# The routed experts' up product in split single precision, full slot tiles first, causal key rows in one product

## The reference

```
q, k, v = x Wq, (x Wdown) Wk_up, (x Wdown) Wv_up      16 heads of 16, rotary on 12 of the 16
x1 = layernorm(x + softmax(causal(q k' / 4)) v)
scores = softmax(x1 gate')                              16 experts, the best two of each token
y = sum over the two chosen experts e of  w_e * ((silu(x1 w1[e]') * (x1 w3[e]')) w2[e]')    176 inner columns
z = the same product with one shared expert of 352 inner columns
out = layernorm(x1 + y + z)
```

## Time and profile before

| | us |
|---|---|
| median of three runs | 795.77 (789.0 to 796.28) |
| the profiled execution | 791.07 |
| its span, first to last instruction | 789.3 |
| PE busy in the span | 705.3 (89%) |
| DVE, ACT, POOL busy | 561.8, 395.3, 242.8 |
| PE's share of the chain that ended last | 71% |

### The profile page before, as it was taken

One profiled execution on the slowest core, in us unless ns is written; L12 is line 12 of the kernel. 1 busy time (PEld: TensorE's weight loads), 2 busy tenths in 40 slices (PEclk: granted clock), 3 DMA queues, 4 the chain that ended last, 5 costly groups with the idle time before them and its releaser, 6 DMA issues.

```text
span 789.3 us, 13246 instructions
## 1 busy us (share of the span) xinstructions
PE 705.3 (89%) x4150; PEld 468.9 (59%) x4151; DVE 561.8 (71%) x1279; ACT 395.3 (50%) x848; POOL 242.8 (31%) x297
## 2 busy tenths in 40 slices
PE   3589899899999999999999999999999799999910
PEld 3577575565766566556645565554477677777700
DVE  6666679978879977786798888753676655555545
ACT  2225465556656566666665777656823222222204
POOL 6426173440081207011511000010166513333332
PEclk9759799999999999999999999999999999999965
DMA  4854215043015101500421274522342133333254
GB/s 138 214 161 112 79 42 147 27 129 90 1 44 146 55 1 42 121 1 1 121 61 64 64 242 161 153 69 56 89 115 98 61 87 103 107 107 107 87 186 159
DMA packets 45096, 75.94 MB, mean 96 GB/s; under 512 B 5695, under 2 KB 23359, under 8 KB 44863
## 3 DMA queue, kind: packets, MB, share of 16 engines
q1 hardware_dynamic: 37423, 57.55, 26.9%
q0 software_dynamic: 4896, 13.67, 5.0%
q10 hardware_dynamic: 2720, 4.00, 1.4%
HBM read 41.91 MB, written 32.93 MB: 95 GB/s over the span
## 4 chain that ended last, share of the span: by engine, by line
PE 71%; DVE 15%; issue 4%; DMA 4%; ACT 3%; ACTq 1%; POOL 1%; SPq 0%; POOLq 0%; DVEq 0%
PE banks_ps L1079 16%; PE banks_ps L1136 15%; PE banks_ps L1116 14%; PE banks_ps L1173 7%; DVE mx L1343 5%; PE banks_ps L1207 5%; PE banks_ps L994 3%; PE banks_ps L1084 2%; PE banks_ps L1186 2%; ACT probs L881 2%; PE banks_ps L1269 1%; PE banks_ps L1195 1%; DVE base L1777 1%; PE banks_ps L1220 1%; DMA q_stack<-m_rows 1%
## 5 line engine op out<-in xcount | busy, mean ns | idle before, releaser
L881 ACT ACTIVATE probs<-banks_ps 128x512 f32<-128x512 f32 (+3 forms) x640 | 302.4, 546 | 185.5 <-PE banks_ps L1116 169.2
L1343 DVE TENSOR_REDUCE mx<-banks_ps 128x1 f32<-128x512 f32 (+3 forms) x576 | 307.6, 593 | 66.1 <-PE banks_ps L1079 65.2
L1079 PE MATMUL banks_ps<-k_stack,q_stack 96*128 96x512 f32 (+3 forms) x832 | 249.8, 364 | 7.1 <-DMA q_stack<-kq_split 3.1
L1116 PE MATMUL banks_ps<-q_stack,k_stack 98*128 98x512 f32 (+3 forms) x640 | 242.1, 397 | 12.1 <-ACT probs L881 6.6
L1079 PEld LDWEIGHTS banks_ps<-k_stack,q_stack 96*128 96x128 f32 x832 | 150.9, 200 | 84.7 <-DVE mx L1343 36.4
L1116 PEld LDWEIGHTS banks_ps<-q_stack,k_stack 98*128 98x128 f32 x640 | 121.9, 194 | 50.5 <-ACT probs L881 28.2
L735 POOL TENSOR_SCALAR_AFFINE_SELECT probs<-probs 128x512 f32<-128x512 f32 x64 | 40.9, 639 | 333.7 <-ACT probs L881 333.5
L1136 PE MATMUL banks_ps<-probs,v_ones 128*17 128x512 f32 (+3 forms) x1280 | 133.9, 536 | 0.9 <-POOL probs L735 0.9
L791 POOL DMA_INDIRECT token_y<-ys,dest x47 | 45.6, 970 | 82.0 <-DVE ys L1753 79.2
L1136 PEld LDWEIGHTS banks_ps<-probs,v_ones 128*17 128x17 f32 x1280 | 29.5, 97 | 65.3 <-issue 38.5
L1337 DVE TENSOR_REDUCE mx<-banks_ps 128x4 f32<-128x512 f32 x64 | 44.2, 691 | 28.7 <-PE banks_ps L1084 27.2
(11 more groups left out here) (180 smaller groups left out, 690.1 us busy)
## 6 DMA issues: line engine op xcount, KB each, us to landing
kq_split<-kq_stage SPq DMA_DIRECT2D x32, 256.0 KB, 3.4
k_stack<-kq_split SPq DMA_DIRECT2D x8, 768.0 KB, 6.7
q_stack<-kq_split SPq DMA_DIRECT2D x32, 192.0 KB, 5.7
xg<-slot_x SPq DMA_DIRECT2D x47, 130.0 KB, 2.2
slot_x<-blank SPq DMA_DIRECT2D x11, 520.0 KB, 6.3
w_up_sb<-w_up SPq DMA_DIRECT2D x16, 352.0 KB
kq_split<-kq_stage SPq DMA_DIRECT2D x32, 128.0 KB, 3.3
x_raw<-xT SPq DMA_DIRECT2D x4, 512.0 KB, 5.5
```

What stands on the lines that cost most here:

```text
L881: nc.scalar.activation(probs[:, s % PROB_BUFS, h, off:CH], score_bank(n)[:, off:CH], ACT.Exp)\
L1079: ins = nc.tensor.matmul(dst[:, at:at + keys], q_stack[0:STACK, u % 4, h, tile * P:(tile + 1) * P], k_stack[0:STACK, pair, kb * CH + k0:kb ...
L1116: nc.tensor.matmul(score_bank(n)[:, off:CH], k_stack[:, 2 * g + h // 2, b * P:(b + 1) * P], q_stack[:, u % 4, h, off:CH], start=True, stop ...
L1343: last = nc.vector.tensor_reduce(mx[:, u % 2, h * TPC + tile, column:column + 1], bank_of(bank)[:, at:at + keys], AX.X, ALU.max)
```

## The change

1. **Up product of the routed loop.** It becomes a split product: six fp32r matmuls of 352 columns in place of two plain f32 ones. ACT copies each expert's up weights (704 columns) to their high part (`high_expert`), POOL writes the low part over the raw ones (`low_expert`): twelve experts at steps of units 14 and 15 (`SPLIT_AT`, after the step's last exponential), four beside items 2, 4, 6 and 8 of the shared expert. DVE makes the low part of each tile's rows (`low_rows`), and PE's up product waits for it.
2. **Memory.** The split weights take twice the room. The raw up weights are loaded in another order and at other steps, the last four during the shared expert; the down weights come in five loads after attention, the last of them (experts 12 to 15, 704 KB) after `experts_ready`, and PE waits for all five before the loop. The shared expert's down weights and the last chunk's input rows are loaded after the last score; their split is by ACT and then by DVE ahead of item 0 (`low_down`), where DVE did all of it beside unit 15. Sums are kept in the rows of x1 (`sum_of`), so `take_shared(b)` waits for the scatters of chunk b.
3. **Full slot tiles first.** The slot order is: tiles that the first 12 token tiles fill for sure, then their partly filled ones, then those the last chunk adds. `early_slots` has more to compute; the expert of each tile is counted in three pieces, beside items 2, 4 and 10, where it was one beside item 8; and the first 9 slot tiles (`SURE`) are loaded without waiting for the last chunk's scatters.
4. **Causal rows at once.** For a unit's own chunk, query tile i has one product over its (i+1)*128 keys: tile 3 in one bank, tiles 2 and 0 in another, tile 1 in a third, each bank with a mask product of 128, 256 and 128 columns.

```diff
-SHARED_BANKS = ((1, 3), (2,))
+OWN_BANKS = ((3,), (2, 0), (1,))
...
+        ends = np.cumsum([(i + 1) * P for i in OWN_BANKS[n]])
+        return [(i, 0, (i + 1) * P, int(end) - (i + 1) * P) for i, end in zip(OWN_BANKS[n], ends)]
...
+    SPLIT_ORDER = (0, 1, 12, 2, 3, 4, 13, 5, 6, 7, 14, 15, 8, 9, 10, 11)
+    EXPERT_UP_AT = tuple(first_step[UNITS - 3] + 3 + 5 * n for n in range(3)) + \
+        tuple(first_step[UNITS - 2] + 1 + 3 * n for n in range(4)) + tuple(first_step[UNITS - 1] + 1 + 2 * n for n in range(5))
+    SPLIT_AT = tuple(first_step[UNITS - 2] + 2 * n + 1 for n in range(6)) + (first_step[UNITS - 1],) + \
+        tuple(first_step[UNITS - 1] + 4 + 2 * n for n in range(5))
+    SPLIT_BESIDE = (2, 4, 6, 8)
...
+        w_up_raw = lay("w_up_raw", late, 0, [P, EXPERTS, 2, KT, 2 * INTER])
+        w_up = lay("w_up_split", late, 0, [P, EXPERTS, 2, KT, 2 * INTER], F32R)
+        w_dn = lay("w_dn_sb", late, 28928, [HALF, EXPERTS, 2, E])
+        yg = lay("yg", late, 0, [P, 2, TOP_K, TPC, E])
+        x_tok_last = lay("x_tok_last", late, 22528, [P, TPC, E])
+        dn_raw = lay("dn_raw", late, 23568, [P, NG, E])
+        shared_dn = [lay("dn_high", late, 24576, [P, NG, E], F32R), lay("dn_low", late, 23568, [P, NG, E], F32R)]
...
+        def sum_of(b):
+            return base_last if b == LAST_C else x1[0][:, b * TPC:(b + 1) * TPC, 0:E]
...
-            def load_expert_up(e):
-                sp.dma_start(w_up[:, e], t["w_up"][:, e]).then_inc(experts_loaded, 16)
+            def load_expert_up(n):
+                e = SPLIT_ORDER[n]
+                sp.dma_start(w_up_raw[:, e, 0], t["w_up"][:, e]).then_inc(up_loaded[n], 16)
...
-            sp.wait_ge(weights_low, 6)
+            sp.wait_ge(pe_scores, GH * NS)
+            sp.dma_start(dn_raw, t["s_dn"]).then_inc(shared_loaded, 16)
             sp.dma_start(x_tok[LAST_C], t["x"][LAST_C * CH:, :].rearrange("(i p) n -> p i n", p=P)).then_inc(tokens_loaded, 16)
-            sp.wait_ge(pe_scores, GH * NS)
-            load_expert_down(2, 6)
-            load_expert_down(6, 10)
-            sp.wait_ge(scattered, 16 * TOP_K * TT)
+            for n in range(4):
+                sp.wait_ge(pe_gate, 2 * n + 1)
+                load_expert_up(EXPERTS - 4 + n)
+                load_expert_down(3 * n, 3 * n + 3)
+            sp.wait_ge(experts_ready, 1)
+            load_expert_down(12, EXPERTS)
+            for c in range(LAST_C):
+                sp.wait_ge(scattered[c], 16 * TOP_K * TPC)
...
+            for j in range(SURE):
+                load(j, j % RING, j)
+            sp.wait_ge(scattered[LAST_C], 16 * TOP_K * TPC)
+            turns = (SLOTS - SURE) // UNROLL
+            with sp.Fori(0, turns) as turn:
+                for k in range(UNROLL):
+                    load(turn * UNROLL + (SURE + k), (SURE + k) % RING, SURE + k)
...
+            def low_expert(n):
+                e = SPLIT_ORDER[n]
+                pool.wait_ge(up_high, n + 1)
+                nc.gpsimd.tensor_tensor(w_up[:, e, 0], w_up_raw[:, e, 0], w_up[:, e, 1].bitcast(F32), ALU.subtract).then_inc(up_low, 1)
...
+                if s - 1 in SPLIT_AT:
+                    low_expert(SPLIT_AT.index(s - 1))
...
+            for n in range(len(SPLIT_AT), EXPERTS):
+                low_expert(n)
             pool.wait_ge(slots_ready, 2)
             scatter(x1[1], EARLY, range(TPC))
...
+            def high_expert(n):
+                e = SPLIT_ORDER[n]
+                act.wait_ge(up_loaded[n], 16)
+                nc.scalar.activation(w_up[:, e, 1], w_up_raw[:, e, 0], ACT.Copy).then_inc(up_high, 1)
...
+                    if h == 3 and s in SPLIT_AT:
+                        high_expert(SPLIT_AT.index(s))
...
+            act.wait_ge(shared_loaded, 16 * 5)
+            nc.scalar.activation(shared_dn[0], dn_raw, ACT.Copy).then_inc(weights_high, 1)
...
+                if n in SPLIT_BESIDE:
+                    high_expert(len(SPLIT_AT) + SPLIT_BESIDE.index(n))
...
-                if masked:
-                    ins = nc.tensor.matmul(dst.rearrange("p (i k) -> p i k", i=TPC), ident_b[:],
-                                           mask_b[:].unsqueeze(1).to_broadcast([P, TPC, P]), start=False, stop=True,
+                if own:
+                    first, last = parts[0][2] - P, parts[-1][3] + parts[-1][2]
+                    ins = nc.tensor.matmul(dst[:, first:last].rearrange("p (i k) -> p i k", k=P), ident_b[:],
+                                           mask_b[:].unsqueeze(1).to_broadcast([P, (last - first) // P, P]), start=False, stop=True,
...
-            def up(n, par, x_of, e):
-                for k in range(KT):
-                    last = nc.tensor.matmul(gate_ps[par][:, 0:2 * INTER], x_of(k), w_up[:, e, k, :],
-                                            start=(k == 0), stop=(k == KT - 1))
+            def up(n, par, e):
+                for m, (k, (a, w)) in enumerate(product(range(KT), PARTS)):
+                    last = nc.tensor.matmul(gate_ps[par][:, 0:2 * INTER], xg_t[:, par, a, k, :], w_up[:, e, 1 - w, k, :],
+                                            start=(m == 0), stop=(m == 3 * KT - 1))
...
-                    pe.wait_ge(experts_loaded, 16 * (EXPERTS + 5))
+                    pe.wait_ge(experts_loaded, 16 * 5)
+                    pe.wait_ge(up_low, EXPERTS)
...
-                pe.wait_ge(xt_copied, j + 1)
+                pe.wait_ge(xt_low, j + 1)
                 if j0 == 0:
                     pe.wait_ge(wide_hidden_done, SHARED)
-                up(j, j0 % 2, lambda k: xg_t[:, j0 % 2, k, :], bass.ds(own, 1))
+                up(j, j0 % 2, bass.ds(own, 1))
...
-                if kb == c and i == 0:
-                    nc.vector.tensor_reduce(mx[:, u % 2, h * TPC:(h + 1) * TPC, c:c + 1],
-                                            bank_of(bank).rearrange("p (i k) -> p i k", i=TPC), AX.X, ALU.max)\
-                      .then_inc(max_done, 1)
-                    return
-                column = kb if kb < c else c + 1
                 for tile, _, keys, at in bank_parts(bank):
-                    last = nc.vector.tensor_reduce(mx[:, u % 2, h * TPC + tile, column:column + 1],
+                    last = nc.vector.tensor_reduce(mx[:, u % 2, h * TPC + tile, kb:kb + 1],
...
+            def low_down():
+                dve.wait_ge(weights_high, 6)
+                nc.vector.tensor_tensor(shared_dn[1], dn_raw, shared_dn[0].bitcast(F32), ALU.subtract).then_inc(weights_low, 1)
...
+            def move_on(at, n):
+                link(nc.vector.tensor_tensor(grid[:, at], place[:, at], along_t(row_of(CAP), n), ALU.is_ge))
+                link(nc.vector.scalar_tensor_tensor(out=grid[:, at], in0=grid[:, at], scalar=float(P),
+                                                    in1=along_t(row_of(JUMP), n), op0=ALU.mult, op1=ALU.mult))
+                link(nc.vector.tensor_tensor(place[:, at], place[:, at], along_t(row_of(AHEAD), n), ALU.add))
+                link(nc.vector.tensor_tensor(place[:, at], place[:, at], grid[:, at], ALU.add))
             def early_slots():
                 wait_read(dve, ("ranks", 0, 0))
-                count_tiles(tiles[:, TILES0, :], tiles[:, N0, :])
-                tiles_before(tiles[:, START0, :], tiles[:, TILES0, :])
-                link(nc.vector.tensor_scalar(tiles[:, AHEAD, :], tiles[:, START0, :], float(P), None, ALU.mult))
-                link(nc.vector.tensor_tensor(place[:, 0:EARLY], place[:, 0:EARLY], along_t(tiles[:, AHEAD, :], EARLY), ALU.add))
+                count_tiles(row_of(TILES0), row_of(N0))
+                link(nc.vector.tensor_scalar(row_of(N1), row_of(N0), float(1 - P), None, ALU.add))
+                count_tiles(row_of(FULL), row_of(N1))
+                tiles_before(row_of(FSTART), row_of(FULL))
+                link(nc.vector.tensor_tensor(row_of(FEND), row_of(FSTART), row_of(FULL), ALU.add))
+                link(nc.vector.tensor_tensor(row_of(MORE), row_of(TILES0), row_of(FULL), ALU.subtract))
+                tiles_before(row_of(PSTART), row_of(MORE))
+                link(nc.vector.tensor_scalar(row_of(PSTART), row_of(PSTART), tiles[:, FEND, EXPERTS - 1:EXPERTS], None, ALU.add))
+                link(nc.vector.tensor_tensor(row_of(PEND), row_of(PSTART), row_of(MORE), ALU.add))
+                link(nc.vector.tensor_scalar(row_of(CAP), row_of(FULL), float(P), None, ALU.mult))
+                link(nc.vector.tensor_scalar(row_of(AHEAD), row_of(FSTART), float(P), None, ALU.mult))
+                link(nc.vector.tensor_tensor(row_of(JUMP), row_of(PSTART), row_of(FEND), ALU.subtract))
+                move_on(slice(0, EARLY), EARLY)
...
+            def experts_of_full():
+                tiles_ended(0, FEND)
+                zero_behind(0)
+            def experts_of_partial():
+                tiles_ended(1, PEND)
+                zero_behind(1)
+                link(nc.vector.tensor_tensor(expert_f[:, 0, :], expert_f[:, 0, :], expert_f[:, 1, :], ALU.add))
+            def experts_of_late():
```

(34 more changed lines are left out.)

169 lines of the change are left out of this document (68 added, 101 removed).

## The result

The changed kernel takes 802.93 us (median of five runs, 801.39 to 805.55) where the kernel before took 795.77: ratio 1.010, 95% interval 1.0066 to 1.0133. The forecast was 788, its range 776 to 802, so the result lies 0.9 above its upper end; 1.010 is on the bound that the prediction drew between no change and slower. Ratios leave out single executions at an unusually low granted clock (one version took 896.73 us once, at 0.731). The profiled execution of the changed kernel takes 802.93 with a span of 801.1; against the 791.07 and 789.3 of the profiled execution before that is 11.8 more, and it divides into four stretches.

The account below looks back on a forecast made before the run. PE was taken as the bound, with 71% of the chain that ended last. 791.07 - 10.0 - 6.0 + 2.7 + 0.9 + 6.3 + 1.7 = 786.7 us, put at 788 because the runs' median lies above the profiled execution; range 776 to 802.

Parts of the forecast that it names:

- the bound that the prediction drew between no change and slower: Whole kernel: one per cent counts as a change, so slower means above 799 against 791.07.
- Into the loop: Passage from attention to routed loop: first up product +6.3 us later, +1.7 for a slowed clock; ends +2 and +12.
- Loop: Routed loop: six 352-column matmuls take 0.97 where the up product takes 1.18, over 47 tiles -10.0 us.
- The rival that DVE bounds the loop: Routed loop: DVE's queue costs a tile 2.65 and PE waits each time, execution 804; chance 0.15.
- Own key blocks: Attention, a unit's own chunk: 0.92 us a head instead of 1.04, counted as -6 us; ends 0 and -11.
- Splits by ACT: Attention units 14 and 15: ACT's high-part copies delay PE, +2.7 us and +0.9 us.

## Why the prediction was wrong

It said -4.4 and the trace says +11.8; the 16.2 between them are 3.1 in attention, 8.75 in the entry, 4.8 in the loop, less 0.5 at the end.

*Into the loop*, the term of +6.3 and +1.7, is the step that failed, and it failed twice. Its path was right: DVE sets the pace, the last down load goes out only behind the list of experts, and PE waits for it. Two prices on that path were wrong. Up to the first down product the sum held: `early_slots` +5.5 against 5.5 measured, `down_shared(0)` at 583.6 against 583.30, an idle time of 6.15 where about 7 was to show. That was partly luck: the new operations took 4.0 where I had 4.5, the subtraction held DVE 1.5 where I had 1.0, and counted from ACT's last copy the down product came 5.5 later, not 6.5.

The first wrong price is that of the POOL subtractions. I charged 2 in all where rows 8 had shown a doubled operation, and wrote beside it what the lock would cost by the Trainium skill's rule, 8. From 567 us on they cost DVE 6.3: 1.5, then 4.75 where three of them met one operation, and nothing for the last. The list of experts was ready at 640.66 instead of 634.4. With DVE doing the last four itself it comes 64.4 us after ACT's last copy, and my 634.4 is 64.1 after that of the kernel before. The Trainium skill (SBUF — State Buffer, SBUF: two separate sides) says that whoever comes first of a GpSimd operation and a DVE operation with two SBUF inputs gets the shared pair of ports for the whole instruction. The trace agrees that DVE is held for all of it, and not with the share that I took from a row in which a POOL mask had held the count 0.40. It goes beyond the rule in that DVE did not get its turn between one subtraction and the next: 5.17 for 0.42.

The second wrong price is the load at the door. I took 4.3 for the last down load by its size; it landed 7.1 after issue, and 7.0 to 7.3 in the three versions in which the gather loads went ahead of it. The gather loads stood behind it in SP's queue, where my working had no transfer at all, and released PE another 0.3 later. Why 704 KB took 7 where 512 had taken 3.5 stays open; the last scatters were under way. The first up product, forecast at 640.2, started at 650.0: 6.3 of the 9.8 is the list, 3.2 the load and the gather load behind it, and 0.3 the transposes and copies on a slow clock. The cure was not a faster load: nothing needed those loads behind the list, or the down weights before the first down product. Changing both gave 7.7, and DVE's subtractions 4.3.

*Loop*, -10.0: the size was right for a tile (2.27 where it was to be 2.28), by two errors that cancel: the up product itself takes 1.05 and not 0.97, and the transposes ahead of it give the rest, 0.14 from their start to the product's (679.25 to 679.39) where it was 0.22. Straight code has all of it, 101.5 for 111.4. The rival that DVE bounds the loop did not come: PE waits for DVE once, 0.2 us at 656.11. What I left out is the turn of PE's loop, which had cost 0.4 us in all and now cost 4.6; the working had no term for it. The time came near the 804 of the rival by other means.

*Own key blocks*, -6: 4.3 by the ratio, with 2.1 to 6.5 for its interval: right in direction, a little less in size. A head takes 1.66 (515.62 to 517.28) where I had 1.63. Stretches at full clock give 0.23 us a unit (six units, 206.62 for 208.02) to 0.39 (three, above), 4 to 6 in all. Some of the difference in attention (3.1) is clock: in the changed kernel's profile two stretches, 130 to 150 and 430 to 440 us, stand at 0.83, which the kernel before has at full clock, while its own unit 14 has one. The later of the two goes with the new blocks: of the twelve profiles that have them ten show a low stretch that begins between 429 and 436 us, of the two without them neither. Unit 12 takes 50.98 with it (49.70 before, 49.41 in a profile of the changed kernel's blocks without it), so it gives back about 1.5 us of the gain. What brings it about was not tested.

*Splits by ACT*, +3.6: 3.0 in unit 14 and 0.7 in unit 15 (38.77 against 38.06), 3.7 in all. Right, and by the mechanism given, though two slips stand in its working: 826 x 704/768 is 0.76, and three times 0.35 is 1.05.

## What to carry to other kernels

Where two engines share ports, look at what the other engine runs at that place. If its queue there is full of operations on SBUF, count each instruction of the first at its whole length, and move the work off rather than about; beside reads of PSUM or an idle engine it cost nothing here. Before a stage whose entry hangs on one result, list every transfer queued behind that result and ask of each whether it needs it: here neither the gather loads nor the first products needed it, and that was worth 7.7 us. Do not read a load's time off its size by two smaller loads from another stretch of the kernel. When matmuls get shorter, look for what they had been hiding on their own engine, such as the turn of a loop.

## What the runs showed of the hardware

- A DVE operation can be held over several GpSimd instructions in a row, 5.17 us over three of 1.67, and a sixteen-wide operation with a single tensor operand was held as well (1.68). DVE's reductions from PSUM beside the same subtractions were not: 0.68 each, as elsewhere.
- Five turns of PE's loop cost 0.4 us in all with tiles of 12 matmul records in 2.49 us, and 4.6 with tiles of 14 in 2.27, most of it in the two tiles behind each turn; the same tiles as straight code have no such cost.
- A gather load of 130 KB lands 2.1 us after issue in the loop, but the first of four behind a load of 704 KB landed after 6.9, with the last scatters under way; five of its sixteen parts were there 2.8 before the last. The 704 KB themselves took 7.0 to 7.3 in four traces, with and without gather loads behind them.
- 352 columns of a split product cost 0.175 us (1.05 for six, 660.67 to 661.72), 0.161 by proportion between 256 and 512 columns.
